# Own buffers for the second half of y, sums over every fourth position, the roots stored from GpSimd's queue, and a new order

## The reference

```python
x = x + tanh(g_xattn[0]) * xattn(layernorm(x), ctx, ctx, Wq, Wk, Wv, Wo, bo, g)
x = x + tanh(g_ffn[0]) * ffn(layernorm(x), w_gate, w_up, w_down)

# the end of xattn: (b, 128 channels, 1024 positions)
out = einsum('bcn,oc->bon', out, Wo) + bo[None, :, None]
norm = maximum(sqrt(sum(out * out, axis=1, keepdims=True)), 1e-12)
return out / norm * g * sqrt(128)

# ffn: bitlinear(x, w) = x @ (round(clip(w / (mean|w| + eps), -1, 1)) * mean|w|).T
return bitlinear(bitlinear(h, w_gate) * bitlinear(h, w_up), w_down)
```

## Time and profile before

| What | Value |
|---|---|
| Median of 3 runs | 1391.26 us |
| Lowest and highest | 1383.13 and 1392.24 us |
| The profiled execution | 1387.74 us |
| Its span on the core | 1385.9 us |
| Mean granted clock of TensorE | 0.977 |
| TensorE busy | 1304.8 us, 94% of the span |
| VectorE, ScalarE, GpSimd busy | 965.7, 624.6, 565.4 us |

### The profile page before, as it was taken

The page is one execution under the profiler, slowest core; times in us unless marked ns, Lnnn a source line. Parts: engine busy times, 40 slices in busy tenths (PEclk is TensorE's granted clock), DMA queues, the critical chain, the costliest instruction groups (busy, mean ns, idle before and its releaser), DMA issues. The chain is left out here.

```text
span 1385.9 us, 29984 instructions
## 1 busy us (share of the span) xinstructions
PE 1304.8 (94%) x12280; PEld 948.9 (68%) x12280; DVE 965.7 (70%) x1343; ACT 624.6 (45%) x879; POOL 565.4 (41%) x357
## 2 busy tenths in 40 slices
PE   5887498899999999999999999999999999999999
PEld 3554285665678657976588757976598757985994
DVE  5986677587888877788778776777568865842230
ACT  3888676564434534354335443454334443420220
POOL 0178732674455462554333632344234331331120
PEclk7998799999999999999999999999999999999999
DMA  9959799999475899787797777967798776657421
GB/s 355 390 199 309 221 298 280 213 224 187 110 163 162 175 203 245 196 179 164 188 206 189 163 177 176 234 155 164 141 232 199 175 166 146 160 140 182 142 89 53
DMA packets 410631, 268.43 MB, mean 194 GB/s; under 512 B 330432, under 2 KB 347200, under 8 KB 410496
## 3 DMA queue, kind: packets, MB, share of 16 engines
q1 hardware_dynamic: 403584, 241.36, 71.0%
q10 hardware_dynamic: 6912, 25.17, 5.7%
HBM read 160.76 MB, written 26.02 MB: 135 GB/s over the span
## 5 line engine op out<-in xcount | busy, mean ns | idle before, releaser
L1126 PE MATMUL ps<-w_dn,inter_buf 128*128 128x512 fp8e4 x1376 | 304.3, 379 | 1.4 <-issue 1.4
L1126 PEld LDWEIGHTS ps<-w_dn,inter_buf 128*128 128x128 f16 x1376 | 134.3, 99 | 156.7 <-issue 1.5
L1814 POOL TENSOR_TENSOR qs<-qs,q_stat 128x1024 f32<-128x1024 f32 x64 | 126.7, 1984 | 162.8 <-DVE q_stat L1623 162.4
L1042 PE MATMUL ps<-zT,w_gu 128*128 128x256 f16 x1664 | 190.1, 275 | 0.1
L1042 PEld LDWEIGHTS ps<-zT,w_gu 128*128 128x128 fp8e4 x1664 | 164.1, 99 | 25.6 <-issue 1.1
L1077 PE MATMUL ps<-w_gu 128*128 128x128 f16 x2880 | 173.4, 219 | 1.5 <-ACT w_gu L1138 0.8
L1077 PEld LDWEIGHTS ps<-w_gu 128*128 128x128 fp8e4 x2880 | 164.9, 98 | 4.0 <-issue 1.8
L1870 POOL TENSOR_TENSOR w_gu<-w_gu 128x512 f32<-128x512 f32 x60 | 82.2, 1371 | 176.2 <-DVE w_gu L1725 132.7
L1725 DVE SCALAR_TENSOR_TENSOR w_gu<-ps,w_gu 128x512 f32<-128x512 f32 x120 | 81.9, 687 | 92.4 <-PE ps L1077 91.6
L1077 PE MATMUL ps<-zT,w_gu 128*128 128x128 f16 x2176 | 132.6, 219 | 0.5 <-DMA w_gu<-forms 0.5
L1077 PEld LDWEIGHTS ps<-zT,w_gu 128*128 128x128 fp8e4 x2176 | 125.1, 98 | 2.4 <-DMA w_gu<-forms 0.7
(11 more groups left out here) (193 smaller groups left out, 2518.6 us busy)
## 6 DMA issues: line engine op xcount, KB each, us to landing
w_gu<-forms SPq DMA_DIRECT2D x158, 256.0 KB, 4.2
ct_raw<-forms SPq DMA_DIRECT2D x52, 256.0 KB, 4.2
w_dn<-in_down_w SPq DMA_DIRECT2D x19, 512.0 KB, 5.8
xb<-in_x ACTq DMA_DIRECT2D x16, 512.0 KB, 5.0
ysq<-r_dram SPq DMA_DIRECT2D x32, 256.0 KB, 4.2
x_dram<-xb SPq DMA_DIRECT2D x16, 512.0 KB, 3.9
fin<-x_dram SPq DMA_DIRECT2D x32, 256.0 KB, 3.6
out<-fin SPq DMA_DIRECT2D x32, 256.0 KB, 3.1
```

The lines of the kernel that those rows point to most:

```text
L1042: last = nc.tensor.matmul(ps[:, rest_bank(g, j), s * T:s * T + T], w_gu[:, w, k, :], zT[:, h, k, :], start=(k == 0 and h == 0), stop=(k == ...
L1126: mm = nc.tensor.matmul(ps[:, down_bank(g, k), :], inter_of(g, j, u % 2, b), w_dn[:, j, hf * 512:hf * 512 + 512], start=(u == 0), stop=(u ...
L1814: nc.gpsimd.tensor_tensor(v, v, q_stat[:, u % 2, 1, :].unsqueeze(2).broadcast_to([P, 2 * HEADS, DH]), ALU.mult).then_inc(q_prob, 1)
```

## The change

- `yev`, `ss`, `get_r`, `x2m` and `x2a` take their buffers from `y_of(i, hf)`. For the second half of the batches from 4 on these are two pieces of `stage_c`; all else stays in `ysq`. `yev` of such halves waits for the x2 of the half two before and no longer for that of the half just before. Its first one waits besides until all weights are rounded, since `stage_c` is one of the buffers for their loads.
- `ss` takes every fourth position as the stationary operand of a matmul (a step of 4 fp32 elements, 16 bytes), so that partition p holds positions 4p to 4p + 3, the row in DRAM is in the order of the positions, and `x2m` reads and writes without a step.
- `put_r` is issued by GpSimd. `r_stored` and `r_in` are one semaphore for each half.
- `WHEN` is another list for all kinds, with the same steps. The stage buffers' list `SLOT` is the same. In the new order `put_r` stands next behind `rs` on GpSimd. The first `gu` step is number 472 where it was 468.

```diff
--- before.py
+++ after.py
@@ -91,251 +91,252 @@
...
-    "yev": [211, 267, 383, 406, 667, 771, 928, 965, 1069, 1130, 1317, 1380, 1507, 1630, 1739, 1810, 1935, 1973,
...
-    "ss": [205, 282, 366, 431, 662, 808, 923, 992, 1106, 1166, 1355, 1411, 1559, 1622, 1756, 1842, 1953, 2018, 2168,
...
+    "yev": [202, 269, 368, 406, 637, 750, 933, 982, 1092, 1138, 1323, 1377, 1525, 1625, 1756, 1792, 1932, 1971,
...
+    "ss": [190, 276, 352, 393, 647, 766, 923, 987, 1110, 1173, 1359, 1405, 1538, 1618, 1769, 1827, 1956, 2012, 2168,
...
-    "put_r": [178, 268, 362, 433, 671, 782, 900, 987, 1092, 1121, 1349, 1402, 1549, 1665, 1772, 1807, 1912, 1975,
...
-    "get_r": [250, 299, 376, 443, 686, 789, 963, 1023, 1097, 1126, 1357, 1407, 1587, 1686, 1779, 1836, 1949, 1981,
...
+    "put_r": [129, 263, 371, 429, 618, 756, 943, 969, 1072, 1156, 1315, 1365, 1578, 1611, 1712, 1824, 1928, 1930,
...
+    "get_r": [172, 305, 383, 453, 714, 803, 940, 1008, 1081, 1191, 1393, 1409, 1623, 1644, 1790, 1841, 1984, 1985,
...
@@ -541,7 +542,7 @@
         qf_hi_s, qf_lo_s, eT_in = sem("qf_hi_s"), sem("qf_lo_s"), sem("eT_in")
         out_ready, y_ready, sq_ready = sem("out_ready"), sem("y_ready"), sem("sq_ready")
         ss_ready, ss_guarded, rs_ready = sem("ss_ready"), sem("ss_guarded"), sem("rs_ready")
-        r_stored, r_in = sem("r_stored"), sem("r_in")
+        r_stored, r_in = ([sem(f"{n}{h}") for h in range(2)] for n in ("r_stored", "r_in"))
         y_scaled, x2_ready, x2_stored = sem("y_scaled"), sem("x2_ready"), sem("x2_stored")
         ln2, rstd2, z_ready = sem("ln2"), sem("rstd2"), sem("z_ready")
         z_hi_s, z_lo_s = sem("z_hi_s"), sem("z_lo_s")
@@ -694,6 +695,12 @@
             else:
                 wait(eng, qf_lo_s, NU * (i - BY_PE) + u + 1)
 
+        def y_of(i, hf):
+
+            if hf == 0 or i < GB * PLAIN:
+                return y, sq
+            return stage_c[:, 0, 0:512], stage_c[:, 0, 512:1024]
+
         def rows_of(i):
             return slice(i * P, i * P + P)
 
@@ -788,13 +795,9 @@
                 x = 7 * s + q
                 sp.dma_start(ring[n % RING], forms[x * P:x * P + P, :]).then_inc(form_in[n % RING], 16)
 
-            def put_r(i, hf):
-                wait(sp, rs_ready, 2 * i + hf + 1)
-                sp.dma_start(r_dram[2 * i + hf, :].rearrange("(p k) -> p k", p=P), rsv[:, hf, :]).then_inc(r_stored, 16)
-
             def get_r(i, hf):
-                wait(sp, r_stored, 16 * (2 * i + hf + 1))
-                sp.dma_start(sq, r_dram[2 * i + hf:2 * i + hf + 1, :].broadcast_to([P, 512])).then_inc(r_in, 16)
+                wait(sp, r_stored[hf], 16 * (i + 1))
+                sp.dma_start(y_of(i, hf)[1], r_dram[2 * i + hf:2 * i + hf + 1, :].broadcast_to([P, 512])).then_inc(r_in[hf], 16)
 
             def st_x2(i, _):
                 wait(sp, x2_ready, 2 * i + 2)
@@ -815,7 +818,7 @@
 
             program({"consts": consts, "wload": wload, "turn_c": turn_c,
                      "turn_k": turn_k, "turn_q": turn_q, "turn_z": turn_z, "turn_zs": turn_zs, "store_form": store_form,
-                     "load_form": load_form, "put_r": put_r, "get_r": get_r, "st_x2": st_x2, "reload": reload,
+                     "load_form": load_form, "get_r": get_r, "st_x2": st_x2, "reload": reload,
                      "st_out": st_out})
 
             sp.wait_ge(x2_stored, 16 * B)
@@ -1013,8 +1016,9 @@
             def ss(i, hf):
                 wait(pe, y_ready, 2 * i + hf + 1)
                 wait_banks(out_free)
+                v = y_of(i, hf)[1].rearrange("c (p k) -> c k p", k=4)
                 for k in range(4):
-                    last = nc.tensor.matmul(ps[:, OUT, k:k + 1], sq[:, k * P:k * P + P], ones, start=True, stop=True)
+                    last = nc.tensor.matmul(ps[:, OUT, k:k + 1], v[:, k, :], ones, start=True, stop=True)
                 last.then_inc(ss_ready, 1)
                 out_free[0] = (ss_guarded, 2 * i + hf + 1)
 
@@ -1296,8 +1300,12 @@
 
             def yev(i, hf):
                 wait(act, out_ready, 2 * i + hf + 1)
-                wait(act, x2_ready, 2 * i + hf)
-                wait(act, ss_ready, 2 * i + hf)
+                before = 2 * i + hf - (1 if 2 * i + hf > 2 * GB * PLAIN else 0)
+                wait(act, x2_ready, before)
+                wait(act, ss_ready, before)
+                if i == GB * PLAIN and hf == 1:
+                    act.wait_ge(wq_done, len(QUANT_OF))
+                v, v2 = y_of(i, hf)
                 wait(act, m_ranged, 3 * i + 3)
                 if hf == 0:
                     if i <= BY_PE:
@@ -1307,9 +1315,9 @@
                 if i == 0:
                     act.wait_ge(s_small, 80)
                 u = y_unit[:, i % 2:i % 2 + 1]
-                nc.scalar.activation(y, ps[:, OUT, :], ACT.Identity, bias=small[:, BO:BO + 1],
+                nc.scalar.activation(v, ps[:, OUT, :], ACT.Identity, bias=small[:, BO:BO + 1],
                                      scale=u).then_inc(y_ready, 1)
-                nc.scalar.activation(sq, ps[:, OUT, :], ACT.Square, bias=small[:, BO:BO + 1],
+                nc.scalar.activation(v2, ps[:, OUT, :], ACT.Square, bias=small[:, BO:BO + 1],
                                      scale=u).then_inc(sq_ready, 1)
 
             def z_hi(i, _):
@@ -1634,14 +1642,12 @@
                 nc.vector.tensor_scalar(ssv[:, hf, :], ps[:, OUT, 0:4], 1e-24, None, ALU.max).then_inc(ss_guarded, 1)
 
             def x2m(i, hf):
-                wait(dve, r_in, 16 * (2 * i + hf + 1))
+                wait(dve, r_in[hf], 16 * (i + 1))
                 wait(dve, y_ready, 2 * i + hf + 1)
                 if i == 0:
                     dve.wait_ge(coef_x, 1)
-                v = y.rearrange("c (k p) -> c k p", k=4)
-                nc.vector.scalar_tensor_tensor(out=v, in0=sq.rearrange("c (p k) -> c k p", k=4),
-                                               scalar=small[:, COEF_X:COEF_X + 1],
-                                               in1=v, op0=ALU.mult, op1=ALU.mult).then_inc(y_scaled, 1)
+                v, r = y_of(i, hf)
+                nc.vector.scalar_tensor_tensor(out=v, in0=r, scalar=small[:, COEF_X:COEF_X + 1], in1=v, op0=ALU.mult, op1=ALU.mult).then_inc(y_scaled, 1)
 
             def ln2_(i, _):
                 wait(dve, x2_ready, 2 * i + 2)
@@ -1816,15 +1822,19 @@
 
             def rs(i, hf):
                 wait(pool, ss_guarded, 2 * i + hf + 1)
-                wait(pool, r_stored, 16 * (2 * i + hf - 1))
+                wait(pool, r_stored[hf], 16 * i)
                 nc.gpsimd.tensor_tensor(rsv[:, hf, :], ssv[:, hf, :], neg_half.broadcast_to([P, 4]),
                                         ALU.pow).then_inc(rs_ready, 1)
+
+            def put_r(i, hf):
+                wait(pool, rs_ready, 2 * i + hf + 1)
+                nc.gpsimd.dma_start(r_dram[2 * i + hf, :].rearrange("(p k) -> p k", p=P), rsv[:, hf, :]).then_inc(r_stored[hf], 16)
 
             def x2a(i, hf):
                 wait(pool, y_scaled, 2 * i + hf + 1)
                 wait(pool, xr_in[i % 2], 16 * (i // 2 + 1))
                 v = xb[:, i % 2, hf * 512:hf * 512 + 512]
-                nc.gpsimd.tensor_tensor(v, v, y, ALU.add).then_inc(x2_ready, 1)
+                nc.gpsimd.tensor_tensor(v, v, y_of(i, hf)[0], ALU.add).then_inc(x2_ready, 1)
 
             def z(i, _):
                 if not ON_DVE <= i < GB * PLAIN:
@@ -1870,7 +1880,7 @@
                 nc.gpsimd.tensor_tensor(v[:, :, 0, :], v[:, :, 0, :], v[:, :, 1, :], ALU.mult).then_inc(pair_muled, 1)
 
             program({"consts": consts, "wquant": wquant, "rstd1": rstd1_, "rstd2": rstd2_,
-                     "qnorm": qnorm, "q32": q32_, "q_lo": q_lo_, "z": z, "z_sum": z_sum, "form": form, "pair_mul": pair_mul, "rs": rs, "x2a": x2a})
+                     "qnorm": qnorm, "q32": q32_, "q_lo": q_lo_, "z": z, "z_sum": z_sum, "form": form, "pair_mul": pair_mul, "rs": rs, "put_r": put_r, "x2a": x2a})
 
 
 def kernel(**inputs):
```

More of the change, by code:

```diff
@@ L93 @@
 WHEN = {
[L94 to L98, removed]
@@ L304 @@
-    "st_out": [958, 1043, 1240, 1260, 1458, 1468, 1498, 1570, 1870, 1894, 2013, 2113, 2313, 2371, 2464, 2465, 2730,
[L305 to L311, removed]
-    "wtotal": [214, 235, 684],
-    "wscale": [225, 230, 689],
-    "consts": [5],
-    "prod": [32],
-    "gains": [54],
@@ new lines @@
+    "turn_q": [491, 550, 677, 715, 804, 844, 884, 946, 980, 1026, 1059, 1077, 1124, 1194, 1279, 1375, 1407, 1493,
+        1510, 1537, 1566, 1703, 1767, 1794, 1878, 1896, 1935, 1950, 2060, 2061, 2147, 2180, 2240, 2304, 2352, 2375,
+        2481, 2491, 2562, 2597, 2637, 2699, 2772, 2773, 2884, 2908, 3017, 3022, 3075, 3108, 3198, 3288, 3321, 3367,
+        3418, 3432],
+    "outp": [158, 159, 160, 161, 252, 253, 268, 270, 325, 326, 338, 345, 377, 378, 379, 382, 608, 610, 611, 635,
[6 rows of a table added]
+    "yev": [202, 269, 368, 406, 637, 750, 933, 982, 1092, 1138, 1323, 1377, 1525, 1625, 1756, 1792, 1932, 1971,
[3 rows of a table added]
@@ new lines @@
```

(28 more changed lines are left out.)

227 lines of the change are left out of this document (105 added, 122 removed), and 203 rows, old and new, of the table WHEN.

## The result

The changed kernel takes 1411.1 us (median of 4 runs, 1409.0 to 1413.4), the kernel before 1389.7 (median of 4, 1383.1 to 1392.2): a ratio of 1.016, 95% interval [1.012, 1.020]. The profiled execution took 1412.2 us with a span of 1410.4.

The account below looks back on a forecast made before the run. From 283 us on the time was taken as TensorE's own work; before that, TensorE waits for others. Terms 0 - 1 + 21 + 3 - 6 + 1 + 1 = +19 us on the 1391.3 us median gave 1410 us, range 1380 to 1424.

Parts of the forecast that it names:

- the case that was taken as the likeliest: Sums of squares: weight loads with the step take twice their time; range 1400 to 1424 us, chance 0.52.
- ss with a step: Sums of squares after 283 us: the 16-byte step doubles TensorE's weight loads, +21 us, bounds 0 and 43.
- The +3 for the front: Before 283 us: 48 more weight loads double, +5 us if all show, taken as +3.
- Own y: Second halves from batch 4 on: removes at most 0.9 us of `ysq` wait after 283 us; taken as 0.
- the -1: `x2m` without a step, six halves before 283 us: about 0.5 us saved each, up to -3, taken as -1.
- The store from GpSimd: Root store in the front: quicker landing gives -6 us (bounds 0 and -12), GpSimd's issue costs +1 (at most +5).
- the gain of 7 us from the landing in batch 1: Batch 1's root store lands in the median 2.5 us instead of 10.5, taking about 7 us off its chain.
- 0, whoever issues: Bound of the store's gain: the landing was late because DMA engines are 93% busy, so GpSimd's issuing gains 0.
- all of what TensorE gains here stays, since nothing later waits: Front, batch 1: TensorE time won by the quicker store landing carries to the end; store gain taken as -6 us.
- The new order: Step list `WHEN`: can add or remove waits after 283 us, between -5 and +8 us, taken as +1.
- a first `gu` near 166: Profile sign in batch 1: with the quicker store, the first `gu` starts before 172 us, around 166.
- no earlier first `gu`: Sign against the store term: if the first `gu` starts no earlier, the store's queue didn't matter.

Follow-up runs that it names:

- the first 8: Kernel before, with the root store issued by GpSimd for the first four batches alone (8 of 32), SyncE for the rest: 1386.7 us, ratio 0.9968.
- the other 24: Kernel before, with the root store issued by GpSimd only for batches from the fifth on (24 of 32): 1391.0 us, ratio 1.0005.
- the idle store: Kernel before, SyncE's store kept, plus a GpSimd store of constants to spare DRAM behind each root, on which nothing waits: 1412.1 us, ratio 1.0154.
- the kernel with the small GpSimd instruction: Kernel before plus a small GpSimd multiplication of constants behind each of 32 roots, no DMA, SyncE's store kept: 1391.3 us, ratio 1.0002.

## Why the prediction held, and where it didn't

1410 us was forecast and 1411.1 measured, by the case that was taken as the likeliest. The largest term was right in mechanism and size; that the rest came out so close is in part luck. The terms, by their own measurements:

- **ss with a step: right, +21 forecast, +21 measured.** Half of the pace of a load without a step was chosen, from the one row of VectorE with such a step. The reason was thin; the experiments put a better one in its place (the 16 bytes). A half goes from 0.81 to 1.68 us (1.6 forecast), the loads from 26.0 to 50.5 us (45 forecast, though twice 26 would be 52).
- **The +3 for the front: the size of the work right, its effect not to be seen.** The sums there do take 3.3 us more. But the term took the doubling as holding at every clock: where the clock was 0.50, a half costs 0.16 us more and not 0.8. And with the step alone the second pair of batches begins no later than before (364.9 us, before 365.7).
- **Own y: right, 0.** Its wait is hidden and its buffer unused, as measured alone.
- **x2m: the mechanism right; the -1 was never measured by itself.** 1144 to 751 ns at the median (743 in `stage_c`), not 0.69 us. The means fall only from 1231 to 1192 and 1077 ns, because some of these instructions are held for up to 3.8 us.
- **The store from GpSimd: wrong in sign, -5 forecast, +9 measured alone.** Two steps of it failed. The first is the gain of 7 us from the landing in batch 1, which was read off one trace: SyncE's unchanged store lands after 3.8 us in other traces, without a faster kernel, so the 10.5 us went by the load on the DMA engines at that moment and cost nothing that is seen. The prediction had this among its bounds (0, whoever issues). The second is "all of what TensorE gains here stays, since nothing later waits": the chain to the first `gu` wasn't shortened, and the wait for z stayed (6.1 and 6.5 us), which the prediction itself had named as next in line. And for the time after 283 us it counted only GpSimd's own time, 1 us for each issue, which is 0.62; it had no term for any other cost of the 32 stores, and what the 9 us are is open.
- **The new order: +1 forecast, not to be told from 0.** The forecast of a first `gu` near 166 failed by 13 us, 8 of them with the new order (179.5 us, against 171.5 for the same code in the old one), and this had no effect on the end. By the prediction's own sign (no earlier first `gu`) the store's queue didn't matter.
- **The sum.** +21 [17, 26] and +9 [6.5, 12.6] would be +30. The change costs 22 [17, 28], and 25 [22, 29] in the old order, so the parts seem to overlap by 6 to 8 us, which these intervals hardly set apart from 0. If they overlap, the longer loads take the place of waits: TensorE stands 23.4 us after 283 us without the step, and 16.4 with it. The prediction's +19 is near 22 since it had the store 14 us too low and the front's 3 us too high and knew no overlap; these errors nearly cancel. The waits after the front were forecast at 5 to 15 us and are 12.8.

**What stays open** is why 32 stores from GpSimd cost 9 us when the first 8 cost nothing (or gain) and the other 24 nothing, and why a store that nothing waits for costs 21. Shown is that it isn't only the path of the roots, and not the long holds of VectorE in the front. GpSimd's own time is ruled out only for 0.2 us a root; a filler as long as the issue would test the rest, though the 8 and the 24 issues that cost nothing speak against it too. What the trace of the idle store has is many small waits of TensorE; a slower landing of neighbouring transfers would make such waits, but that was not tried by itself. Nor do the waits of one execution settle it: in the kernel with the small GpSimd instruction, whose time is that of the kernel before, they come to 13.7 us, and in that with the store from GpSimd alone to 14.9.

## What to carry to other kernels

Where one engine is full, ask of each edit first how it changes the length of that engine's own instructions: here 24 us of longer weight loads decided the sign, and what freed VectorE or a buffer bought nothing that could be measured. Lay a weight operand out so that each 16 bytes give at least two of its elements, or reorder on the other side, where an engine has time to spare. A wait that is shortened in a starved front is worth only what reaches the next fixed point (here the first product of the second pair of batches); look there, before crediting it to the end. And look at that point, and at the wait itself, in a second trace with the same front: one wait of 10.5 us was 3.8 in the next.

## What the hardware showed that I had not expected

- A 128x128 fp32 weight load with a step of 16 or 32 bytes keeps TensorE's load side busy for 243 and 247 ns (50.5 and 51.4 us for 208) at the full clock against 125 without (26.0); with 8 bytes it is 131 (27.3). At a granted clock of 0.50 eight pairs take 2.00 against 1.84 us.
- A VectorE instruction with two inputs in SBUF may be held not behind one GpSimd instruction but behind an unbroken row of them, 6.33 us where it took 2.06. Such holds stand in kernels without a DMA from GpSimd too (7.71 us for 128x1 elements in the run with own y alone, again beside an unbroken row of GpSimd instructions), but more often in those with it: two to five of 4 us or longer in a trace, against none or one.
- 32 stores of 2 KB from GpSimd, on which nothing waits, cost 21 us of 1389, though GpSimd spends only 0.62 us on each and is busy 41% of the span.
- The same 2 KB store on SyncE's queue was read back after 10.5 us when issued at 128.75 us into full DMA engines, and after 3.8 when issued at 132.15, when they had begun to empty.
